# Another order of the first tiles in a two-layer low-rank adapter kernel on TensorE

## The reference

```python
# layer 0: A, B of 64 adapters, rank 16
x = x + (x @ B[id0].T) @ A[id0].T
# layer 1: a dense layer with bias, and adapters of rank 16 among 32, scaled by 2
x = x + x @ W.T + b + ((x @ As[id1]) @ Bs[id1]) * 2
```

## Time and profile before

| what | value |
|---|---|
| median of 3 runs | 1412.16 us |
| the profiled execution, its own time | 1413.14 us |
| its span in the trace | 1411.1 us |
| TensorE busy | 1368.4 us (97%), 5928 matmuls |
| DVE busy | 951.0 us (67%) |
| ACT busy | 552.6 us (39%) |
| DMA queue of SP | 62.7% of 16 engines' span |
| memory read and written | 249.70 MB, 72.35 MB |

### The profile page before, as it was taken

How to read it: one execution, slowest core, us unless ns; L and a number is a source line. 1 busy time by engine, 2 the same in 40 slices (tenths; PEclk the granted TensorE clock), 3 DMA queues, 4 the chain that set the end, 5 groups by cost and what they waited for, 6 DMA issues and landing times.

```text
span 1411.1 us, 16438 instructions
## 1 busy us (share of the span) xinstructions
PE 1368.4 (97%) x5928; PEld 1116.9 (79%) x5928; DVE 951.0 (67%) x1143; ACT 552.6 (39%) x666; POOL 86.4 (6%) x179
## 2 busy tenths in 40 slices
PE   3888999999999999999999999999999999999999
PEld 2676777888888888888888888888888888888887
DVE  5768876888875666667855676666875566655662
ACT  4443423446334432345523442344633443223321
POOL 2000001000000001010000000110010000000000
PEclk8899999999999999999999999999999999999999
DMA  9768995999973666577853556575973366545542
GB/s 351 217 228 300 356 368 193 324 361 345 329 260 128 220 223 205 182 258 241 290 181 123 183 193 241 167 246 204 326 240 125 124 225 227 192 157 196 197 150 82
DMA packets 101332, 323.15 MB, mean 229 GB/s; under 512 B 13508, under 2 KB 15044, under 8 KB 100996
## 3 DMA queue, kind: packets, MB, share of 16 engines
q1 hardware_dynamic: 95188, 307.68, 62.7%
q0 software_dynamic: 6064, 14.43, 3.6%
HBM read 249.70 MB, written 72.35 MB: 228 GB/s over the span
## 4 chain that ended last, share of the span: by engine, by line
PE 87%; DVE 4%; DMA 4%; ACT 2%; issue 1%; SPq 1%; DVEq 0%; ACTq 0%
PE acc L695 26%; PE acc L696 26%; PE acc L697 26%; DMA w_two<-w 4%; PE acc L675 2%; PE down_ps L640 2%; PE down_ps L641 2%; PE up_ps L653 2%; DVE w_one L887 1%; DVE bg_raw L946 1%; ACT w_hi L740 1%; DVE resident L946 1%; DVE x_lo L919 0%; DMA bg_raw<-x 0%; ACT x_hi L758 0%
## 5 line engine op out<-in xcount | busy, mean ns | idle before, releaser
L695 PE MATMUL acc<-x_hi,w_hi 128*128 128x512 f32 x1792 | 703.0, 392 | 6.6 <-DVE x_lo L919 3.7
L696 PE MATMUL acc<-x_lo,w_hi 128*128 128x512 f32 x1792 | 700.5, 391 | 0.0
L697 PE MATMUL acc<-x_hi,w_lo 128*128 128x512 f32 x1792 | 700.2, 391 | 0.0
L740 ACT ACTIVATE w_hi<-w_one 128x1024 fp32r<-128x1024 f32 x224 | 237.0, 1058 | 544.5 <-PE acc L697 491.1
L896 DVE TENSOR_TENSOR w_lo<-w_one,w_hi 128x1024 fp32r<-128x1024 f32 x224 | 274.2, 1224 | 227.7 <-ACT w_hi L740 227.0
L695 PEld LDWEIGHTS acc<-x_hi,w_hi 128*128 128x128 f32 x1792 | 337.9, 189 | 82.8 <-issue 6.9
L696 PEld LDWEIGHTS acc<-x_lo,w_hi 128*128 128x128 f32 x1792 | 338.0, 189 | 73.1 <-issue 1.0
L697 PEld LDWEIGHTS acc<-x_hi,w_lo 128*128 128x128 f32 x1792 | 337.4, 188 | 71.6
L772 ACT ACTIVATE sums<-acc 128x512 f32<-128x512 f32 x96 | 56.9, 593 | 192.3 <-PE acc L697 186.5
L979 DVE SCALAR_TENSOR_TENSOR sums<-acc,bias_sb,sums 128x512 f32<-128x512 f32 x128 | 95.5, 746 | 25.5 <-PE acc L675 25.1
L919 DVE TENSOR_TENSOR x_lo<-x_stage,x_hi 128x1024 fp32r<-128x1024 f32 x80 | 96.0, 1219 | 2.9 <-ACT x_hi L758 2.7
(11 more groups left out here) (60 smaller groups left out, 668.7 us busy)
## 6 DMA issues: line engine op xcount, KB each, us to landing
w_one<-w_sums SPq DMA_DIRECT2D x120, 512.0 KB, 4.3
w_one<-w SPq DMA_DIRECT2D x104, 512.0 KB, 5.5
bg_raw<-x SPq DMA_DIRECT2D x84, 512.0 KB, 6.1
x_stage<-x SPq DMA_DIRECT2D x68, 512.0 KB, 5.1
out<-sums SPq DMA_DIRECT2D x128, 256.0 KB, 3.6
w_two<-w SPq DMA_DIRECT2D x40, 512.0 KB, 8.1
w_sums<-w_one SPq DMA_DIRECT2D x40, 512.0 KB, 5.6
resident<-x SPq DMA_DIRECT2D x32, 512.0 KB, 8.1
```

The costliest lines, as they stand in the source:

```text
L695: pe.matmul(ps[:, :], w_hi[ws][:, c, :], hi, start=(c == 0), stop=False)
L696: pe.matmul(ps[:, :], w_hi[ws][:, c, :], lo, start=False, stop=False)
L697: mm = pe.matmul(ps[:, :], w_lo[ws][:, c, :], hi, start=False, stop=(c == H - 1))
L740: act.activation(w_hi[s % W_PARTS][:, :, :], w_one[s % W_ONES][:, :, :], ACT.Copy).then_inc(w_hi_ready, 1)
```

## The change

The names on the left are those of the code.

- **SP**: the two gathers of the first down weights (`down_raw`) stand behind chunk 0 alone; chunk 1 and the two early chunks follow them.
- **Chunks 4 and 5** of sequence 1 are split into parts 4 and 5 of x, so six chunks in all (`e < 12`) use x's parts; the gathers of `a0_raw` on POOL and `a1_raw` on SP wait until 12 halves are used.
- **Before step 0**, ACT and DVE split the up weights before chunk 4 and W 0 behind all chunks of sequence 1; the down weights and the first chunk of sequence 0 are split before the first share is added; DVE adds share v + 1 before it splits part v of x; W 1 is made behind all four parts.
- **`split_rank_x`** signals its first copy, so that DVE can subtract beside the second, and `rank_x_copied` tells TensorE of the second.
- **In a step**, DVE adds the share of the first chunk of `ups(s)` before it splits W, and the second chunk's right behind that. The copy of a1 on ACT in step 3 stands behind the share.
- **The images** use `down_ps` and `image_ps` in turn; the next projection down into that bank waits for all four.
- **B0's chunks** go up one step later (8, 9, 11, 12 for 7, 8, 10, 11), with the loads and sums of product 2 that read them; product 1's first sum and split come a step earlier.

```diff
--- before.py
+++ after.py
@@ -53,20 +53,20 @@
 
 def load_at(p):
 
-    return (1, 2, 5, 6) if p % PRODUCTS == 2 else (0, 1, 3, 5)
+    return (2, 3, 5, 6) if p % PRODUCTS == 2 else (0, 1, 3, 5)
 
 
 def sum_at(p):
 
     if p == 1:
-        return (5, 5, 6, 7)
-    return {1: (2, 3, 5, 6), 2: (2, 3, 6, 7)}.get(p % PRODUCTS, (1, 3, 5, 6))
+        return (4, 5, 6, 7)
+    return {1: (2, 3, 5, 6), 2: (3, 4, 6, 7)}.get(p % PRODUCTS, (1, 3, 5, 6))
 
 
 def split_at(p):
 
     if p == 1:
-        return (6, 6)
+        return (5, 6)
     return {0: (3, 5), 1: (4, 5), 2: (4, 5)}.get(p % PRODUCTS, (2, 4))
 
 
@@ -115,7 +115,7 @@
     found = [2, 3] if s == 0 else []
     if i == 0:
         found += [16 * g + 4 * A0 + r for r, at in enumerate((1, 2, 4, 5) if g else (4, 4, 5, 5)) if at == o]
-    found += [16 * g + 4 * B0 + r for r, at in enumerate((7, 8, 10, 11)) if at == s % PER_GROUP]
+    found += [16 * g + 4 * B0 + r for r, at in enumerate((8, 9, 11, 12)) if at == s % PER_GROUP]
     if i == 2:
         found += [16 * g + 4 * A1 + r for r, at in enumerate((1, 3, 5, 7)) if at == o]
     if i == 6 and g + 1 < GROUPS:
@@ -358,6 +358,7 @@
         down_copied = sem("down_copied")
         down_added = sem("down_added")
         rank_x_hi_ready = sem("rank_x_hi_ready")
+        rank_x_copied = sem("rank_x_copied")
         rank_x_ready = sem("rank_x_ready")
         rank_loaded = sem("rank_loaded")
         rank_hi_ready = sem("rank_hi_ready")
@@ -400,9 +401,12 @@
 
         def down_parts(e):
 
-            if e < 8:
+            if e < 12:
                 return x_hi[e // 2][:, e % 2, :], x_lo[e // 2][:, e % 2, :]
             return bg_hi[e % 3][:, :], bg_lo[e % 3][:, :]
+
+        def image_bank(j):
+            return down_ps if j % 2 else image_ps
 
         def rank_x_of(n):
             return rank_x[0 if n % 2 else 1 + n // 2 % 2]
@@ -507,13 +511,13 @@
 
             sp.dma_start(ids_sb[:, 0, :], ids0).then_inc(ids_loaded, DMA)
             sp.dma_start(ids_sb[:, 1, :], ids1).then_inc(ids_loaded, DMA)
-            for d in (0, 1):
-                load_raw("down", d)
-            for d in (2, 3):
-                load_early(d)
+            load_raw("down", 0)
             sp.wait_ge(ids_loaded, 2 * DMA)
             sp.dma_start(down_raw[0][:, :, :], adapter(0, 1, b0).rearrange("u p c r -> (u p) c r")).then_inc(first_down_loaded, DMA)
             sp.dma_start(down_raw[1][:, :, :], adapter(1, 1, a1).rearrange("u p c r -> (u p) c r")).then_inc(first_down_loaded, DMA)
+            load_raw("down", 1)
+            for d in (2, 3):
+                load_early(d)
             for r in range(CH):
                 load_resident(0, 1, r)
             sp.dma_start(identity_sb[:, :], identity).then_inc(identity_loaded, DMA)
@@ -538,6 +542,8 @@
                     load_x(p + 1, load_at(p + 1).index(o))
                 if s + W_ONES < STEPS:
                     load_w(s + W_ONES)
+                if s == 1:
+                    sp.wait_ge(bg_used, 12)
                 if s in (1, 2):
                     for n in range(4 * s - 4, 4 * s):
                         sp.dma_start(a1_raw[:, n, :, :], adapter(1, n, a1).rearrange("u p c r -> (u p) c r"))\
@@ -605,6 +611,7 @@
             pool.wait_ge(ids_loaded, 2 * DMA)
             load_up(0)
             load_down(0)
+            pool.wait_ge(bg_used, 12)
             for n in range(NB):
                 pool.dma_start(a0_raw[:, n, :, :], adapter(0, n, a0_down).rearrange("u p c r -> (u p) c r"))\
                     .then_inc(a0_loaded, DMA)
@@ -632,6 +639,8 @@
                     pe.wait_ge(down_ready, turn(n) + 1)
                     if turn(n):
                         pe.wait_ge(down_added, turn(n))
+                    if turn(n) == 2:
+                        pe.wait_ge(image_ready, 4)
                 for u in range(2):
                     pe.wait_ge(bg_ready, 2 * d + u + 1)
                     c = 2 * k + u
@@ -645,6 +654,7 @@
                 if r == 0:
                     pe.wait_ge(up_ready, v // 4 + 1)
                     pe.wait_ge(rank_x_ready, turn(n) + 1)
+                    pe.wait_ge(rank_x_copied, turn(n) + 1)
                 for u in range(2):
                     e = 2 * v + u
                     if e >= 2:
@@ -656,9 +666,9 @@
             def make_image(j):
                 pe.wait_ge(across_ready, 1)
                 pe.wait_ge(b1_rows_loaded, NB * DMA)
-                if j:
-                    pe.wait_ge(image_ready, j)
-                pe.matmul(image_ps[:, :], across, rows[:, T * j:T * (j + 1)], start=True, stop=True).then_inc(image_done, 1)
+                if j >= 2:
+                    pe.wait_ge(image_ready, j - 1)
+                pe.matmul(image_bank(j)[:, :], across, rows[:, T * j:T * (j + 1)], start=True, stop=True).then_inc(image_done, 1)
 
             def add_rank(s):
                 g, i, o = where(s)
@@ -668,6 +678,7 @@
                 if o == 0:
                     pe.wait_ge(rank_ready, rank_number(g, i) + 1)
                     pe.wait_ge(rank_x_ready, turn(2 * g + side) + 1)
+                    pe.wait_ge(rank_x_copied, turn(2 * g + side) + 1)
                 if i == 4:
                     pe.wait_ge(copied, copied_before(s) + 1)
                 elif i != 6:
@@ -775,7 +786,7 @@
 
                 wait_for_down_source(act, d)
                 for e in (2 * d, 2 * d + 1):
-                    if e >= 11:
+                    if e >= 15:
                         act.wait_ge(bg_used, e - 2)
                     act.activation(down_parts(e)[0], down_source(e), ACT.Copy).then_inc(bg_hi_ready, 1)
 
@@ -795,7 +806,7 @@
                 else:
                     act.wait_ge(first_down_loaded, 2 * DMA)
                 if turn(n):
-                    act.wait_ge(down_added, turn(n))
+                    act.wait_ge(bg_used, 16 * turn(n))
                 act.activation(down[:, :, 0, 0, :], down_raw[0][:, :, :], ACT.Copy)
                 act.activation(down[:, :, 0, 1, :], down_raw[1][:, :, :], ACT.Copy, scale=SCALE1).then_inc(down_hi_ready, 1)
 
@@ -803,6 +814,7 @@
                 act.wait_ge(bg_used, 16 * (turn(n) + 1))
                 if turn(n):
                     act.wait_ge(rank_x_ready, turn(n))
+                    act.wait_ge(rank_x_copied, turn(n))
                 act.activation(rank_sum[:, :], down_ps[2 * R:4 * R, :], ACT.Copy).then_inc(down_copied, 1)
 
             def split_rank_x(n):
@@ -812,8 +824,8 @@
                 if n % 2 == 0 and n >= 4:
                     act.wait_ge(rank_done, 32 * (n // 2 - 1))
                 x_rank = rank_x_of(n)
-                act.activation(x_rank[0:2 * R, :], rank_sum[:, :], ACT.Copy)
-                act.activation(x_rank[2 * R:4 * R, :], rank_sum[:, :], ACT.Copy).then_inc(rank_x_hi_ready, 1)
+                act.activation(x_rank[0:2 * R, :], rank_sum[:, :], ACT.Copy).then_inc(rank_x_hi_ready, 1)
+                act.activation(x_rank[2 * R:4 * R, :], rank_sum[:, :], ACT.Copy).then_inc(rank_x_copied, 1)
 
             def split_rank(g, i):
                 m = rank_number(g, i)
@@ -827,18 +839,18 @@
             split_down(1)
             split_chunk(2)
             split_chunk(3)
-            split_chunk(4)
             split_up(0)
-            split_w(0)
-            for d in (5, 6, 7):
+            for d in (4, 5, 6, 7):
                 split_chunk(d)
             copy_down(1)
             split_rank_x(1)
+            split_w(0)
+            split_down(0)
+            first, second = downs(0)
+            split_chunk(first)
             for r in range(CH):
                 split_x(0, r)
-            split_down(0)
-            for d in downs(0):
-                split_chunk(d)
+            split_chunk(second)
             for s in range(STEPS):
                 g, i, o = where(s)
                 p = PRODUCTS * g + i
@@ -848,10 +860,6 @@
                     split_w(s + 1)
                 if s >= 1 and where(s - 1)[1] == 1:
                     copy(s - 1)
-                if s == 3:
-                    act.wait_ge(a1_loaded, NB * DMA)
-                    act.activation(a1_cols.rearrange("p (c n r) -> p c n r", c=C, n=NB),
-                                   a1_raw[:, :, :, :].rearrange("p n c r -> p c n r"), ACT.Copy).then_inc(a1_ready, 1)
                 if p + 1 < PRODUCTS * GROUPS:
                     for r in range(2):
                         if o == split_at(p + 1)[r]:
@@ -864,6 +872,10 @@
                     split_chunk(d)
                 if s and s in RANK_X_AT:
                     split_rank_x(RANK_X_AT[s])
+                if s == 3:
+                    act.wait_ge(a1_loaded, NB * DMA)
+                    act.activation(a1_cols.rearrange("p (c n r) -> p c n r", c=C, n=NB),
+                                   a1_raw[:, :, :, :].rearrange("p n c r -> p c n r"), ACT.Copy).then_inc(a1_ready, 1)
                 if s in UP_SPLIT:
                     split_up(UP_SPLIT[s])
                 if (i, o) in RANK_SPLIT:
@@ -1007,21 +1019,26 @@
```

(37 more changed lines are left out.)

## The result

The changed kernel is slower: 1422.13 us (median, 1421.14 to 1423.98) against 1412.08, a ratio of 1.0071 with a 95% interval of 1.0054 to 1.0089. I had forecast 1404.9.

The account below looks back on a forecast made before the run. Short ACT and DVE chains bind to about 110 us, then transfers; of 11.5 us lead at step 9, 7.2 survive. 1413.14 less 7.2 is 1405.9 for the profiled execution, 0.98 above the median, so 1404.9; range 1399.5 to 1410.

Parts of the forecast that it names:

- Bounds: Whole kernel: TensorE full after 240 us; short ACT and DVE chains bind to about 110, then transfers, DMA 0.98 busy.
- Start to the first share: Before step 0: first matmul at 12.4 instead of 13.22, 0.8 us; first share at 26.7 instead of 34.94.
- Share to the end of the first step: Front to the first step's end: alternating additions and splits spend the 8 us lead; end at 53.2 to 53.9, gain 2.3.
- Steps 4 to 8: Waits for additions, a1's copy, up weights and the coupling's bank vanish: 5.3 plus 3.9 us; TensorE 11.5 early at step 9.
- What of it survives: Behind step 8: transfers follow the making of W 8, 6.4 us early; 6.4 - 1.5 + 1.0 + 1.3 leaves 7.2 us.
- The term of +1.3: In 110 to 212 us: 1.3 us won once, the addition no longer between a late W and its split.
- The 1.5 for B0's load: B0 a step later pushes one chunk's load of 512 KB into the full stretch, costing 1.5 us.
- Steady steps: The 48 projections behind step 23: DVE waits for the projection before W's split, 1.5 us to spare; no effect.
- (c): Steady steps: DVE's in-order wait for the projection makes W's split late and stops TensorE each time; slower, 1429; chance 0.04.
- (a): In 110 to 212 us transfers don't bind; TensorE keeps its 11.5 us lead: 1399 to 1402, chance 0.22.
- my case: Main expectation: transfers set the pace behind about 110 us, so 7.2 us survive: 1403 to 1407, chance 0.50.
- the three that I had named as refuting: Wrong if x's third part comes well before 46, idle in 110 to 212 doesn't grow, or steady steps wait for w_lo.

Follow-up runs that it names:

- e11: e5 with SP's first transfers in the order of the kernel before (chunks 0 to 3, then the down weights): 1398.41 us, ratio 0.9891.
- e5: On e1, another order before step 0: share 0 added at once, x's parts split between additions, down weights and chunk 8 after share 3: 1398.13 us.
- e1: The changed kernel with additions to raw (loaded) chunks back behind the making of W, resident chunks still added first: 1404.5 us, ratio 0.9926.
- e8: The kernel before with one thing alone: additions to resident chunks ahead of the split of W: 1411.06 us, ratio 0.9987.
- e2: The changed kernel with all additions of shares behind the making of W, and product 1's first sum and split at their old steps: 1411.18 us, ratio 0.9981.
- e7: e1 with B0's chunks back in their old steps, and product 2's loads and sums too: 1404.25 us, ratio 0.9938.
- e6: The changed kernel, DVE's order kept, with SP issuing a raw chunk's load ahead of the step's W: 1405.97 us, ratio 0.9951.
- e9: e5 with SP issuing a raw chunk's load ahead of the step's W: 1400.54 us, ratio 0.9902.

## Why the prediction was wrong

- **Bounds.** Right that nothing behind 240 us is to be won and that two regimes meet at 110 us. That a lead of TensorE isn't kept whole behind 110 us came true as well. But the 0.98 alone did not tell what bounds the stretch: with the loads late the engines are 0.90 busy and TensorE idles more.
- **Start to the first share.** Share at X = 27.3 (predicted 26.7), clock kept over chunk 4. First matmul 13.03 in this trace, not 12.4: chunk 1, issued at 4.95, reached ACT at 10.35, 5.4 us where I took 4.1. The fit of DMA: Bandwidth & Descriptors in the Trainium skill ("Anatomy of one DMA") gave 3.2, so it was further off than the row; it is a fit of transfers that GpSimd issues, and this one was issued by SP, as one load of several in the air. The first matmul is no steady reading, though: nine traces with this order of loads have it at 11.98 to 13.46, 12.6 on average, four with the order of before at 13.03 to 13.22. So the 0.8 was nearly right there, but it does not reach the first share, which e11 has as early as e5 (TensorE takes it up at 27.63 and 27.66); nor does it show in the time.
- **Share to the end of the first step.** Right: first product 35.60 (34.9), third part 46.35 (46.7), waits of 2.1 us for each part, step 1 at 52.90 (53.2 to 53.9). e5 shows that the alternation was the cause.
- **Steps 4 to 8.** The direction is right and the size a little low: TensorE reaches step 9 13.8 us early where nothing waits there (e1, 112.94 against 126.74; 13.2 at step 10, where both kernels have projected up the same number of chunks), and 11.2 early behind its first wait of 2.65 in the changed kernel; predicted 11.5. As separate gains the terms are not additive: e8 alone wins 1.8 us, since the up weights' wait grows, while much the same edit is worth 6.7 on top of the rest (e1 against e2).
- **What of it survives.** Here lies the failure. The step said: "Recovered are 1.0 ... and 1.3 once, since the addition no longer stands between a W that arrived late ... and the split that TensorE needs." It took DVE's wait for w_two as the only transfer on its path and credited the addition's move. The addition has a transfer of its own, the raw chunk's, and in before it came 0.9 us late only because it stood behind the making of W, a later point by several us. I checked the new place against TensorE's projection alone. The term of +1.3 should have been a price of 17 to 20 us (e1 against the changed kernel).
- The same step's other part, that only the lead at the making of W 8 survives (6.4 of 11.5), was right, and nearly so in size: in e1 W 8 is made 7.7 us early (102.29 against 110.03), TensorE is 13.2 early at step 10, and 7.5 are left at step 24; the time is 9 us shorter (1413.62 to 1404.5; 10 by the ratio). The table in the last section has the other runs. The 1.5 for B0's load isn't seen in the time (e7).
- **Steady steps.** Right: behind 240 us no wait for w_lo, 1170.5 of 1171 us busy. All seven waits for raw loads lie before 230 us. That the loads are early behind it because the DMA engines are only 0.64 busy is argued, not tested.
- **Rivals.** None held the event. (c) had the right place, an addition in order ahead of the split, and the right sign, but the wrong thing waited for (the projection, in the steady steps), and 0.04. It asked whether DVE is late, not whether each operand is there. (a) would have TensorE keep all of its lead; e1 doesn't (13.2 us at step 10, 7.5 at step 24), which speaks for my case there.
- **Signs.** None of the three that I had named as refuting came: the third part was not well before 46, the idle time in 110 to 212 did grow, and no steady step waits for w_lo. What differed was what I had written beside them: the idle time grew by 10.5 us, not 3 to 5, and the releaser on DVE was the raw load, not w_two. A growth past 5 us should have been among the signs of being wrong.

## What to carry to other kernels

When an instruction is moved ahead on an engine that runs in order, price each thing it waits for at the new place, the loads first: a transfer that was never seen waiting may have been hidden by just those instructions that it now overtakes. If the engine's next products also trigger the loads, look for a closed loop; its turn against the time of the same work on the bound engine says whether it sets the pace, and it can be broken in either order, the engine's (e1) or the queue's (e6). Where the loads of a stretch are issued by the work itself, follow a change to the event that issues the first of them (here W 8): that lead, and not the bound engine's, was what lasted.

## What the runs showed that I had not expected

- How early TensorE is behind the stretch follows how early W 8 was made, within 2.2 us, over leads of TensorE from 2.8 to 19.1 us. The loads are issued by the work, so they moved with it, and the DMA engines were busier before the stretch instead (0.74 in 80 to 110 in e5 against 0.58 before). Each row is one trace, in us earlier than in the trace of before (W 8 made 110.03, step 10 133.15, step 24 217.63), and no run moved W 8 alone, so this is a reading and not a test. The changed kernel, with its loop, does not follow it.

| run | W 8 made | step 10 begins | step 24 begins |
|---|---|---|---|
| e2 | 1.1 | 5.7 | 1.5 |
| e8 | 2.8 | 2.8 | 3.0 |
| e7 | 6.4 | 7.8 | 8.2 |
| e1 | 7.7 | 13.2 | 7.5 |
| e9 | 13.5 | 19.1 | 11.3 |
| e5 | 13.5 | 19.1 | 13.0 |
| e11 | 13.5 | 19.1 | 14.4 |
| changed | 8.0 | 10.7 | 9.1 late |

- With the loop in place the DMA engines were less busy, 0.90 in the stretch, and the single loads in it still took 8.07 and 8.80 us: a late issue is not made up by an emptier queue.
- Issuing each raw chunk's load of 512 KB ahead of the two of W on SP (e6) was worth 16 to 17 us (1422.13 to 1405.97, 1.0071 to 0.9951).
